# Feed forward of a cross-attention layer: four groups as one stream with two sets of buffers, inverse deviations on GpSimd

## The reference

```python
y  = layernorm(y_in + cross_out @ out_w.T + out_b) * ln2_g + ln2_b   # cross_out has its value bias added first
h  = gelu(y @ ffn_w1.T + ffn_b1)                                      # 128 -> 512
z  = layernorm(y + h @ ffn_w2.T + ffn_b2) * ln3_g + ln3_b             # 512 -> 128
x  = x + z
```

## Time and profile before

| | us |
|---|---|
| median of 3 runs | 3696.54 (3695.92 to 3699.76) |
| the profiled execution | 3696.36 |
| its span | 3694.6 |
| of that the feed forward | 114.6 |

### The profile page before, as it was taken

The page is one execution under the profiler, slowest core; times in us unless marked ns, Lnnn a source line. Parts: engine busy times, 40 slices in busy tenths (PEclk is TensorE's granted clock), DMA queues, the critical chain, the costliest instruction groups (busy, mean ns, idle before and its releaser), DMA issues. The chain is left out here.

```text
span 3694.6 us, 68033 instructions
## 1 busy us (share of the span) xinstructions
PE 3361.8 (91%) x26619; PEld 1979.3 (54%) x26619; DVE 2414.8 (65%) x5544; ACT 1949.4 (53%) x2681; POOL 1535.3 (42%) x1207
## 2 busy tenths in 40 slices
PE   5769999999998578689999999999999998879998
PEld 3655666666655366445544555555455554655555
DVE  3446777777777344377777777777777776563333
ACT  3324666666665422366666666666666664432222
POOL 1023343333331000067777777777777776210000
PEclk7778999999999668789999999999999999979999
DMA  1003333333331000111011111111111100010000
GB/s 54 1 21 74 78 74 76 75 78 74 75 79 29 0 2 24 38 49 36 22 34 36 36 36 36 37 36 36 36 36 36 36 26 3 1 62 11 1 1 12
DMA packets 90496, 139.23 MB, mean 38 GB/s; under 512 B 14464, under 2 KB 67776, under 8 KB 89408
## 3 DMA queue, kind: packets, MB, share of 16 engines
q1 hardware_dynamic: 90176, 134.87, 13.5%
HBM read 94.41 MB, written 1.05 MB: 26 GB/s over the span
## 5 line engine op out<-in xcount | busy, mean ns | idle before, releaser
L2081 ACT ACTIVATE arena<-banks,arena 128x512 f32<-128x512 f32 x832 | 560.5, 687 | 478.2 <-PE banks L1874 478.2
L1899 PE MATMUL banks<-arena 128*128 128x512 f32 x1664 | 803.9, 603 | 2.7 <-ACT arena L2088 2.7
L1833 POOL TENSOR_TENSOR arena<-arena 128x1024 f32<-128x1024 f32 x256 | 603.9, 2359 | 165.8 <-ACT arena L2088 164.6
L1080 DVE TENSOR_REDUCE arena<-banks 128x1 f32<-128x512 f32 (+1 forms) x896 | 529.4, 627 | 185.2 <-PE banks L965 179.9
L1983 DVE TENSOR_TENSOR banks<-arena,banks 128x512 f32<-128x512 f32 x640 | 444.4, 694 | 243.2 <-ACT arena L2081 223.2
L1177 ACT ACTIVATE arena<-banks 128x1024 f32<-128x1024 f32 (+1 forms) x448 | 424.7, 964 | 315.2 <-PE banks L986 312.2
L2000 DVE TENSOR_TENSOR arena<-arena,banks 128x1024 f32<-128x1024 f32 (+1 forms) x448 | 507.1, 1133 | 1.6 <-PE banks L1889 1.2
L2088 ACT ACTIVATE arena<-arena 128x1024 f32<-128x1024 f32 (+1 forms) x448 | 443.0, 989 | 12.1 <-DVE arena L2000 11.9
L1899 PEld LDWEIGHTS banks<-arena 128*128 128x128 f32 x1664 | 289.9, 190 | 222.7 <-issue 202.2
L1873 PE MATMUL banks<-arena 128*128 128x512 bf16 x832 | 316.7, 381 | 0.0
L1872 PE MATMUL banks<-arena 128*128 128x512 bf16 x832 | 316.5, 380 | 0.0
(11 more groups left out here) (345 smaller groups left out, 5348.5 us busy)
## 6 DMA issues: line engine op xcount, KB each, us to landing
arena<-in_ctxT SPq DMA_DIRECT2D x64, 800.5 KB, 5.5
arena<-arena SPq DMA_DIRECT2D x768, 50.0 KB, 2.2
arena<-in_ctx SPq DMA_DIRECT2D x32, 768.0 KB
arena<-in_m2w SPq DMA_DIRECT2D x3, 2048.0 KB, 12.5
arena<-in_xw SPq DMA_DIRECT2D x1, 2048.0 KB, 7.7
weights<-in_weights SPq DMA_DIRECT2D x1, 1918.0 KB, 7.5
arena<-in_ctx SPq DMA_DIRECT2D x32, 32.5 KB
arena<-in_m1w SPq DMA_DIRECT2D x1, 1024.0 KB, 6.3
```

The costliest lines, as they stand in the source:

```text
L1080: eng.tensor_reduce(o, s, AX, ALU.max).then_inc(a_max, 1)
L1833: eng.tensor_tensor(part, part, tiles, ALU.add).then_inc(sums, 1)
L1899: eng.matmul(c.ps[:, R_MIX + v % 2, :], ctxn[:, b, kt * D:(kt + 1) * D], st[:, v % 2, kt, :], start=kt == 0, stop=kt == KT - 1).then_inc(m ...
L2081: eng.activation(st[:, v % 2, kt, :], c.ps[:, n % SB, :], ACT.Identity, bias=hide[:, kt, v // 2:v // 2 + 1])\
```

## The change

The feed forward is rewritten as one stream. All tiles of a group are moved together where they can be: the inputs by two copies of 128x512 (`oT` with the value bias, `yT` with the output bias), the normalized and turned tiles by two copies (`x2T` with scale and bias of the norm as columns, `x2Tb` with the bias of the second layer added, for the residual). Every buffer has two sets, chosen by `g % 2`, and each kind of PSUM result has two banks. TensorE's order puts the projection of group g+2 between the second and the third hidden product of group g, and the transposes of group g+1 ahead of the output products of group g. The residual is added by a fifth product with the identity. The norms read PSUM directly. The inverse deviations come from GpSimd, by an addition and a power, and GpSimd also adds the last bias row to `x` ahead of time (`xb`). The last norm, its scale and the addition to `x` are two fused operations on VectorE. Four bias and scale rows leave `rows`, and four columns come into `weights`.

```diff
     def pe(eng):
-        for g in range(GROUPS):
-            wait_if(eng, s["x_ready"], g * G)
+        def proj(g):
+            eng.wait_ge(s["o_copied"], g + 1)
+            eng.wait_ge(s["y_copied"], g + 1)
+            wait_if(eng, s["normed2"], G * (g - 1))
             for j in range(G):
-                eng.wait_ge(s["o_copied"], nth(g, j))
-                eng.matmul(A_(j), oT[:, j, :], c.W("c_out"), start=True, stop=False)
-                eng.matmul(A_(j), c.xT[:, g * G + j, :], c.C("ident"), start=False, stop=True).then_inc(s["proj"], 1)
+                w = slice(j * P, (j + 1) * P)
+                eng.matmul(pair(PROJ + g % 2, j), oT[:, g % 2, w], c.W("c_out"), start=True, stop=False)
+                mm = eng.matmul(pair(PROJ + g % 2, j), yT[:, g % 2, w], c.C("ident"), start=False, stop=True)
+            mm.then_inc(s["proj"], 1)
+        def turn(g):
+            eng.wait_ge(s["normed2"], G * g + G)
...
+        def hidden(g, f):
+            if f == 0:
+                eng.wait_ge(s["x2T"], g + 1)
+            wait_if(eng, s["hidden"], g * FU + f - 1)
...
+        def results(g):
+            eng.wait_ge(s["x2Tb"], g + 1)
+            eng.wait_ge(s["hidden"], (g + 1) * FU)
+            wait_if(eng, s["centred"], G * (g - 1))
             for j in range(G):
...
+                eng.matmul(pair(OUT + g % 2, j), x2Tb[:, g % 2, w], c.C("ident"), start=True, stop=False)
+                for f in range(FU):
+                    mm = eng.matmul(pair(OUT + g % 2, j), hT[:, g % 2, f, w], c.W("ffn2", f * D, (f + 1) * D), start=False,
+                                    stop=f == FU - 1)
+            mm.then_inc(s["out_psum"], 1)
+        proj(0)
+        proj(1)
+        turn(0)
+        for g in range(GROUPS):
+            hidden(g, 0)
+            hidden(g, 1)
+            if g + 2 < GROUPS:
+                proj(g + 2)
+            hidden(g, 2)
+            hidden(g, 3)
+            if g + 1 < GROUPS:
+                turn(g + 1)
+            results(g)
     def act(eng):
+        inputs(0)
+        inputs(1)
+        turned(0)
         for g in range(GROUPS):
-            wait_if(eng, s["x_ready"], g * G)
...
+            gelu(g, 0)
+            if g + 2 < GROUPS:
+                inputs(g + 2)
+            for f in range(1, FU):
+                gelu(g, f)
+            if g + 1 < GROUPS:
+                turned(g + 1)
+    def pool(eng):
+        def rstd(n, var, mv, out, g):
+            eng.wait_ge(s[f"mean_var{n}"], G * g + G)
+            eng.tensor_tensor(var[:, g % 2, :], mv[:, g % 2, :, 1], c.eps[:].to_broadcast([P, G]), ALU.add)\
+               .then_inc(s[f"var{n}"], 1)
+            eng.wait_ge(s[f"var{n}"], g + 1)
+            eng.tensor_tensor(out[:, g % 2, :], var[:, g % 2, :], c.power[:].to_broadcast([P, G]), ALU.pow)\
+               .then_inc(s[f"rstd{n}"], 1)
+        def bias_x(g):
+            wait_if(eng, s["x_ready"], G * (g - 1))
+            eng.tensor_tensor(xb[:, g % 2], c.x[:, g * G:(g + 1) * G, :],
+                              c.R("ln3_b").unsqueeze(1).to_broadcast([P, G, D]), ALU.add).then_inc(s["x_biased"], 1)
+        bias_x(0)
+        rstd(2, var2, mv2, rstd2, 0)
+        bias_x(1)
+        rstd(2, var2, mv2, rstd2, 1)
+        for g in range(GROUPS):
+            if g + 2 < GROUPS:
+                rstd(2, var2, mv2, rstd2, g + 2)
+            rstd(3, var3, mv3, rstd3, g)
+            if g + 2 < GROUPS:
+                bias_x(g + 2)
     def dve(eng):
...
+        def norm3(g):
             for j in range(G):
+                eng.wait_ge(s["mean_var3"], nth(g, j))
+                eng.scalar_tensor_tensor(out=t[:, g % 2, j, :], in0=pair(OUT + g % 2, j), scalar=mv3[:, g % 2, j, 0:1],
+                                         in1=c.R("ln3_g"), op0=ALU.subtract, op1=ALU.mult).then_inc(s["centred"], 1)
+            eng.wait_ge(s["rstd3"], g + 1)
+            eng.wait_ge(s["x_biased"], g + 1)
             for j in range(G):
+                eng.wait_ge(s["centred"], nth(g, j))
+                eng.scalar_tensor_tensor(out=c.x[:, g * G + j, :], in0=t[:, g % 2, j, :], scalar=rstd3[:, g % 2, j:j + 1],
+                                         in1=xb[:, g % 2, j, :], op0=ALU.mult, op1=ALU.add).then_inc(s["x_ready"], 1)
+        for g in range(2):
+            measure(2, g, PROJ, "proj", st2, mv2)
+            norm2(g)
+        for g in range(GROUPS):
+            if g + 2 < GROUPS:
+                measure(2, g + 2, PROJ, "proj", st2, mv2)
+                norm2(g + 2)
+            measure(3, g, OUT, "out_psum", st3, mv3)
+            norm3(g)
```

More of the change, by code:

```diff
@@ L1213, in feed_forward @@
     k = Carver(c)
[L1214 to L1220, removed]
@@ L1221, in feed_forward @@
-    Y_ = lambda j: c.ps[:, 4 + j, 0:P]
-    def pe(eng):
-        for g in range(GROUPS):
-            wait_if(eng, s["x_ready"], g * G)
-            for j in range(G):
-                eng.wait_ge(s["o_copied"], nth(g, j))
-                eng.matmul(A_(j), oT[:, j, :], c.W("c_out"), start=True, stop=False)
-                eng.matmul(A_(j), c.xT[:, g * G + j, :], c.C("ident"), start=False, stop=True).then_inc(s["proj"], 1)
[L1230 to L1235, removed]
-            for j in range(G):
[L1237 to L1240, removed]
@@ L1242, in act @@
-    def act(eng):
-        for g in range(GROUPS):
-            wait_if(eng, s["x_ready"], g * G)
[L1245 to L1253, removed]
@@ L1255, in dve @@
-    def dve(eng):
-        for g in range(GROUPS):
[L1257 to L1271, removed]
@@ L1273, in feed_forward @@
-    m.engines = dict(pe=pe, dve=dve, act=act)
+    FU = F0 // P
+    oT, yT = k.f32(2, G * P), k.f32(2, G * P)
+    n2 = k.f32(2, G, D)
+    x2T, x2Tb = k.f32(2, G * P), k.f32(2, G * P)
+    hT = k.f32(2, FU, G * P)
+    xb, t = k.f32(2, G, D), k.f32(2, G, D)
+    b2 = k.f32(1)
+    st2, mv2, var2, rstd2 = k.f32(2, G, 6), k.f32(2, G, 2), k.f32(2, G), k.f32(2, G)
+    st3, mv3, var3, rstd3 = k.f32(2, G, 6), k.f32(2, G, 2), k.f32(2, G), k.f32(2, G)
+    s = {n: c.sem(f"ff_{n}") for n in (
+        "o_copied", "y_copied", "b2_made", "proj", "stats2", "mean_var2", "var2", "rstd2", "normed2", "turned", "x2T", "x2Tb",
+        "hidden_psum", "hidden", "out_psum", "stats3", "mean_var3", "var3", "rstd3", "centred", "x_biased", "x_ready")}
@@ new lines, in act, with inputs, turned, gelu @@
+    def act(eng):
+        def inputs(g):
+            wait_if(eng, s["proj"], g - 1)
+            eng.activation(oT[:, g % 2, :], grp(c.o, g), ACT.Identity, bias=c.W("c_bv")).then_inc(s["o_copied"], 1)
+            eng.activation(yT[:, g % 2, :], grp(c.xT, g), ACT.Identity, bias=c.W("c_out_bc")).then_inc(s["y_copied"], 1)
+        def turned(g):
+            eng.wait_ge(s["turned"], g + 1)
+            wait_if(eng, s["hidden_psum"], (g - 1) * FU)
+            eng.activation(x2T[:, g % 2, :], c.ps[:, TURN + g % 2, :], ACT.Identity, scale=c.W("ln2_gc"), bias=c.W("ln2_bc"))\
+               .then_inc(s["x2T"], 1)
+            eng.wait_ge(s["b2_made"], 1)
+            wait_if(eng, s["out_psum"], g - 1)
+            eng.activation(x2Tb[:, g % 2, :], c.ps[:, TURN + g % 2, :], ACT.Identity, scale=c.W("ln2_gc"), bias=b2)\
+               .then_inc(s["x2Tb"], 1)
+        def gelu(g, f):
+            eng.wait_ge(s["hidden_psum"], g * FU + f + 1)
+            wait_if(eng, s["out_psum"], g - 1)
+            eng.activation(hT[:, g % 2, f, :], c.ps[:, HIDDEN + f % 2, :], ACT.Gelu, bias=c.W("ffn_b1", f, f + 1))\
+               .then_inc(s["hidden"], 1)
+        inputs(0)
[9 more added lines that the diff above has]
+                turned(g + 1)
@@ L1274, in feed_forward @@
+    m.engines = dict(pe=pe, dve=dve, act=act, pool=pool)
     m.after = [(s["x_ready"], PAIRS)]
```

43 lines of the change are left out of this document (38 added, 5 removed).

## The result

The changed kernel takes 3644.23 us (median of 4 runs, 3639.75 to 3645.25), against 3696.23 for the kernel before (3688.09 to 3699.76). The ratio is 0.986, with a 95% interval of 0.985 to 0.988. It is faster, as forecast; the median lies 6 us above the predicted 3638, 1.2 above the forecast's own range of 3632 to 3643 and inside the wider one up to 3652.

What follows compares the result with a forecast made beforehand. The order of the work, not its amount, was taken to bound the feed forward. Groups and tail, 22.5 + 12.1 + 17.9 + 4.1 = 56.6 against 114.6, gain 58.0; with 0.6 from loads, 3638.0 us, range 3632 to 3643, wider to 3652.

Steps and rivals of the forecast that it cites:

- First group: Feed forward, group 0, from input copies to the end of its output products: 22.5 us.
- projection, 8 products or 1.8: First group on TensorE, behind the input copies: eight products at full clock, 1.8 us, done at 1192.5.
- Second group: Feed forward, group 1, all at full clock: 12.1 us, with TensorE busy 10.3 of them.
- Last two groups: Feed forward, groups three and four, with no projection left: 8.95 us each, 17.9 together.
- Tail: End of the feed forward: last statistics, inverse deviation and four final operations, 4.1 us with hand-overs.
- VectorE and GpSimd hidden in full groups: VectorE's 8.2 us per full group lie beneath TensorE's 12.1; GpSimd's addition costs nothing or 0.1.
- Table loads: Feed forward's 20 loads of 1.28 us become one, hidden; Exp's load in linear attention costs nothing, at most 1.28.
- Loads at the start: Start of the program: 254 KB less to load, 0.6 us gained, or none if bytes don't set the landing.
- Clock: TensorE in the feed forward: full clock from 1202.7 on; at half clock all along, the time would be 3669.
- rival of a swinging clock: Feed forward: TensorE's clock does not hold, pausing between groups as PSUM banks cycle; 3638 to 3669 us, 10%.
- Linear attention: The next stage, 89.4 us before: no change taken, 4 us kept both ways for where its clock rises.
- Signs: Expected profile: linear attention about 58 us earlier, output products 12 then 9 apart, full clock, one Gelu load, TensorE's waits.

Runs made afterwards that it cites:

- early tables: The changed kernel with two tiny activations more on ScalarE, loading the Gelu and Exp tables ahead of their use; median 3636.76 us, ratio 0.9838.
- second set of runs: The changed kernel measured once more, with no edit; median 3640.06 us, ratio 0.9848 against the kernel before.

## Why the prediction was right, point by point

**What bounds the stage** was right. The order, not the amount of work, bounded it: the same operations in serial order gain 3.9 of 114.5.

**First group**, 22.5 forecast, 24.2 measured (1194.75 to 1218.96). The failed term is "projection, 8 products or 1.8": it ran at half clock and took about 3.5. I had let the clock fall during TensorE's stand behind the two projections; it had fallen ahead of them (0.65 from 1194.7 to 1196.2, 0.50 from 1196.2 to 1201.9). The normalization reads PSUM in 1.36, not 1.11, and x2T takes 0.78, not 0.69. Transposes at full clock gave 0.5 back. That the first hidden product runs at half clock and hides the table load was right here, and by chance. The clock fell right ahead of it (1.00 from 1202.8 to 1204.8, 0.83 from 1204.8 to 1205.7, then 0.50), though TensorE had stood only 1.39 and 0.87, with the transposes between. In four other kernels it stayed at full clock, with early tables even behind stands of 2.33 and 0.87. So the length of a stand, by which the prediction set the clock, doesn't tell where it falls; what decides it stays open.

**Second group**, 12.1 forecast and 12.22 measured, with its two stands of TensorE where they were said to be. **Last two groups** 8.95 each forecast, 9.15 and 9.2 measured. **Tail** 4.1, and 4.0. The sum was 56.6, and it is 58.8. The gain of the stage was forecast as 58.0 and is 55.8.

**VectorE and GpSimd hidden in full groups**: right. 8.2 of 12.1 would leave 3.9; 2.6 more were taken without any effect. The statistics read PSUM in 0.89, against 0.86 from SBUF.

**Table loads.** No load between Gelus: right, one in the stage. "Cost nothing, at most 1.28" for Exp's load in linear attention: it cost the 1.28. The step that failed is that the load would lie where ScalarE stands; it comes behind the wait.

**Loads at the start**: 0.6 forecast. VectorE starts at 15.94 here and at 15.50 to 16.06 in the twelve profiles with the smaller arrays, at 16.30 and 16.33 in the two with the larger: about 0.5.

**Clock**: full from the projection of group 2 on, 1.00 in both middle windows, so the rival of a swinging clock did not come true outside the first group. By the rule of the Trainium skill that stands beside it (TensorE: Matmul & The Clock Gate, "A second HAM failure mode: psum-queue depth-cycling") it would have; the trace of the middle groups, which alternate between two PSUM banks of each kind, doesn't show it.

**Linear attention**: 90.5, within the 4 each way that were kept. Over all profiles it is 89.3 to 93.7, with the same code apart from the load.

**The 6 us between forecast and median** can be placed in the profiled execution alone, which took 7.0 more than its 3637.8. The stage began 6.1 later than forecast (5.5 later than before, in place of 0.6 earlier) and took 2.2 more. Linear attention gave back 0.4 in spite of Exp's load, at a clock of 0.68 in place of 0.66, and what follows 1.0. So most of the miss is scatter ahead of the stage, and whether a median comes within 2 us of the forecast, as in the second set of runs, or within 6 is in part luck. Why the cross attention's clock is 0.97 in one execution and 0.99 in another stays open.

**Signs.** Output products of the first two groups start 12.22 apart and then 9.15, the one Gelu load and the waits were there, and no transposes waited for VectorE in the middle groups. Linear attention began 50 us earlier, at 1253.6, and not 58: 5.5 of the difference is the late start.

## What to carry to other kernels

Where no engine works half of a stage, price the order and not the operations: here the new operations alone gained 4 us, and the order, on top of them, 52. An operation that costs nothing in a serial order can be dear in an overlapped one, as Ln and Exp with their table loads were (2 against 22.6 us), so the two belong together. When the last few us of a stage are at stake, look at its length over several profiles and at its neighbours as well: a clock that falls elsewhere can take back what an edit gives, and one profile doesn't explain a median.

## What the runs showed of the hardware

VectorE's fused operations with two SBUF inputs wait while GpSimd reads SBUF: 2.14 for four in place of 1.14, beneath an addition of 1.27. The normalization, whose data come from PSUM, does not wait: it takes 1.36 beneath the same addition (1202.67 to 1203.94 in the changed kernel) and 1.37 without it (1206.74).

Keeping TensorE busy ahead of a stage moved its slow stretch and didn't remove it: with three unused products the two projections ran at full clock, and then the third projection, or the first hidden products, at half.
